# Postponed GpSimd and ScalarE work, and seven runs of unread bf16 products on TensorE

## The reference

```
x = x + gnn0(layernorm(x), adj)     # cosine scores of all pairs, tanh, exp, times adj, rows normalised, times x, times W
x = x + ffn0(layernorm(x))          # 16 experts, the two best per token, silu(x w1) * (x w2), times w3
x = x + gnn1(layernorm(x), adj)     # two steps of top-p attention, below
x = x + ffn1(layernorm(x))          # routed by the mean of all tokens, two of 8 experts, gelu, layer norm
```

```
R = (adj + I) / rowsum;  Xf = Xa = X
for n in range(2):
    q, k  = Xa @ W1.T @ W2.T, Xa @ W3.T
    probs = softmax(q @ k.T)                  # 2048 x 2048
    A     = the largest probs of each row up to a sum of 0.9, renormalised
    Xf, Xa = R @ Xf, A @ Xa
    Z    += Xf @ U1[n].T + Xa @ U2[n].T
out = layernorm(X + Z) * ln_g + ln_b
```

## Time and profile before

| what | value |
|---|---|
| median of 3 runs | 877.64 us (876.28 to 877.75) |
| the profiled execution's own time | 879.34 us |
| its span | 877.6 us |
| PE busy | 718.9 us, 82% |
| PEld busy | 530.0 us, 60% |
| DVE busy | 665.1 us, 76% |
| ACT busy | 484.5 us, 55% |
| POOL busy | 277.1 us, 32% |
| mean granted clock of PE | 0.911 of full speed |

### The profile page before, as it was taken

The page is one execution under the profiler, slowest core; times in us unless marked ns, Lnnn a source line. Parts: engine busy times, 40 slices in busy tenths (PEclk is TensorE's granted clock), DMA queues, the critical chain, the costliest instruction groups (busy, mean ns, idle before and its releaser), DMA issues.

```text
span 877.6 us, 15527 instructions
## 1 busy us (share of the span) xinstructions
PE 718.9 (82%) x5089; PEld 530.0 (60%) x5091; DVE 665.1 (76%) x2281; ACT 484.5 (55%) x723; POOL 277.1 (32%) x584
## 2 busy tenths in 40 slices
PE   4999999768999566799999989678778797886294
PEld 2455555427999543477777678465345675786263
DVE  6758677733444377889983499999899999999757
ACT  4877686304555326456555276467696775822153
POOL 3410421336666305400000034051432576770000
PEclk9999999787999869799999999797998997988788
DMA  8764000075887400000000000000000001101001
GB/s 152 118 98 77 26 17 10 26 172 154 230 229 236 160 1 1 0 2 1 1 1 2 1 1 2 1 2 1 0 1 1 1 2 47 51 1 33 0 1 48
DMA packets 47367, 41.94 MB, mean 48 GB/s; under 512 B 7376, under 2 KB 44112, under 8 KB 47280
## 3 DMA queue, kind: packets, MB, share of 16 engines
q1 hardware_dynamic: 29488, 19.95, 8.2%
q0 software_dynamic: 11456, 14.62, 8.0%
q10 hardware_dynamic: 6336, 6.32, 3.0%
HBM read 39.69 MB, written 9.57 MB: 56 GB/s over the span
## 4 chain that ended last, share of the span: by engine, by line
DVE 34%; PE 20%; issue 4%; ACT 4%; POOLq 1%; DVEq 1%; POOL 0%; ACTq 0%
DVE big L1595 6%; PE bank L2138 5%; PE bank L2042 5%; DVE cand L1513 4%; PE bank L2121 4%; DVE rm L1353 3%; DVE hacc L1508 3%; DVE big L1584 2%; DVE cand L1359 2%; DVE cand L1534 2%; PE bank L2315 2%; DVE big L1581 2%; DVE top L1529 2%; ACT big L1868 1%; PE bank L2327 1%
## 5 line engine op out<-in xcount | busy, mean ns | idle before, releaser
L2121 PE MATMUL bank<-ident,big 128*128 128x128 f32 x512 | 82.6, 311 | 31.3 <-DVEq L1618 21.9
L1868 ACT ACTIVATE big<-bank 128x512 f32<-128x512 f32 x128 | 71.0, 597 | 52.5 <-PE bank L2121 51.7
L2121 PEld LDWEIGHTS bank<-ident,big 128*128 128x128 f32 x512 | 63.3, 157 | 59.1 <-DVEq L1618 22.9
L2042 PE MATMUL bank<-kk,qq 64*128 64x512 f32 x256 | 78.8, 734 | 19.8 <-ACT big L1838 19.2
L1838 ACT ACTIVATE big<-bank,negm 128x2048 f32<-128x2048 f32 x32 | 62.7, 1958 | 47.1 <-DVE fsc L1645 36.8
L2049 PEld LDWEIGHTS bank<-parts,adjT 128*128 128x128 bf16 x1536 | 86.6, 98 | 3.0 <-issue 2.1
L2049 PE MATMUL bank<-parts,adjT 128*128 128x128 bf16 x1536 | 87.9, 219 | 0.6 <-DVE xn L1438 0.6
L1595 DVE SCALAR_TENSOR_TENSOR big<-big,st 128x2048 f32<-128x2048 f32 x32 | 75.2, 2388 | 5.2 <-PE bank L2121 5.2
L399 POOL DMA_INDIRECT ys_scratch<-big,parts x62 | 60.0, 967 | 33.2 <-ACT big L754 23.4
L844 PE MATMUL bank<-big,xn 128*128 128x512 f32 x128 | 62.2, 608 | 5.7 <-DVE big L546 5.7
L828 PE MATMUL bank<-xnT 128*128 128x512 f32 x128 | 62.0, 609 | 2.3 <-DVE xnT L535 2.3
(11 more groups left out here) (380 smaller groups left out, 1517.4 us busy)
## 6 DMA issues: line engine op xcount, KB each, us to landing
big<-in_L_ffn_w_dram SPq DMA_DIRECT2D x93, 128.0 KB
big<-in_adj_dram POOLq DMA_DIRECT2D x8, 512.0 KB, 7.3
big<-xs_scratch ACTq DMA_DIRECT2D x31, 132.0 KB
kk<-in_adj_dram POOLq DMA_DIRECT2D x4, 512.0 KB, 8.1
qq<-in_adj_dram POOLq DMA_DIRECT2D x4, 512.0 KB, 10.0
xs_scratch<-hacc SPq DMA_DIRECT2D x9, 132.0 KB
xs_scratch<-hacc ACTq DMA_DIRECT2D x8, 132.0 KB
res<-in_x_dram SPq DMA_DIRECT2D x4, 256.0 KB, 6.3
```

Of the source, the lines that this page charges most:

```text
L1868: nc.scalar.activation(MT[:, 4 * q:4 * q + 4, s * P:(s + 1) * P], bank[:, 5 + q % 2, :].rearrange("p (j i) -> p j i", j=4), ACT.Copy).then ...
L2042: nc.tensor.matmul(bank[:, c, :], qq[lo:lo + DA, (g * G + s) * P:(g * G + s + 1) * P], kk[lo:lo + DA, c * CH:(c + 1) * CH], start=True, st ...
L2121: mm = nc.tensor.transpose(bank[:, 5 + q % 2, j * P:(j + 1) * P], mk[:, s, jt * P:(jt + 1) * P], ident[:, :])
```

## The change

It has two parts.

**Postponed work.** `load_y(act, 1)` stands behind ACT's copies of the weights and ahead of that of the row sums. POOL's split of quarter `q` waits for both flags of group `q` as well, and its additions of `lnb` for those of group 4 (tiles 0 to 7) and group 5 (tiles 8 to 15). `take_pv(g)` waits for the quarter that it overwrites, no longer for all four.

**Unread products.** `keep_busy(b, times)` multiplies the bf16 identity with 512 columns of the bf16 adjacency into bank `b`, over and over; nobody reads the result. It is called seven times, 135 products in all.

```
+        def keep_busy(b, times):
+            for _ in range(times):
+                nc.tensor.matmul(bank[:, b, :], identb[:, :], adjT[:, 0, 0:CH], start=True, stop=True)
...
                 take_y(MB - 1)
-                load_y(act, 1)
                 ch.link(nc.scalar.activation(rs[:, 0:1], ones[:, 0:1], ACT.Exp))
...
+                load_y(act, 1)
                 act.wait_ge(rsum_done, NC + 1)
...
                 mm.then_inc(rsum_done, 1)
+                pe.wait_ge(y_out, 2 * MB)
+                pe.wait_ge(c_id, NT + 1)
+                keep_busy(7, 18)
...
                     pool.wait_ge(ab_part, 3 * q + 3)
+                    pool.wait_ge(flags_up, 2 * (q + 1))
...
                 for t in range(NT):
+                    if t % (NT // 2) == 0:
+                        pool.wait_ge(flags_up, 2 * (NC + 1 + t // (NT // 2)))
                     nc.gpsimd.tensor_tensor(res[:, t, :], res[:, t, :], lnb[:, :], ALU.add).then_inc(c_resb, 1)
...
                 def take_pv(g):
-                    if g == 0:
-                        act.wait_ge(ab_fin, NC)
+                    if g % 2 == 0:
+                        act.wait_ge(ab_fin, g // 2 + 1)
...
+                keep_busy(7, 14)
                 for c in range(NC):
                     turn_x(0, c)
...
                 make_ab(3)
+                pe.wait_ge(ab_part, 3 * 3)
+                keep_busy(4, 13)
                 logits(0, 1, 1)
                 flag_sum(0)
+                keep_busy(4, 12)
...
                         turn_h(1)
+                        keep_busy(2, 20)
                     if g < NG:
                         flag_sum(NG + g)
...
-                for i in range(2, len(XS)):
+                for i in range(2, len(XS) - 1):
                     turn_h(i)
+                keep_busy(6, 34)
+                turn_h(len(XS) - 1)
...
+                keep_busy(6, 24)
                 pe.wait_ge(d_w1, 4)
                 up(0)
```

## The result

| | before | the change |
|---|---|---|
| median, us (runs) | 876.96 (4; 875.99 to 877.75) | 869.40 (4; 866.73 to 871.06) |
| ratio, 95% interval | | 0.991, 0.989 to 0.993 |
| profiled execution, us; its span | 879.34; 877.6 | 871.06; 869.3 |
| mean granted clock of PE | 0.911 | 0.936 |
| PE busy, of the span | 718.9 (82%) | 743.8 (86%) |

The kernel became faster, by 7.6 us, where 8.9 were worked out and 868.7 was forecast. PE is busy for longer, since it now does unread work, in a shorter span. Lines of the code lie a little further down after the change (masking L1605 for L1595, logits L2052 for L2042, turns of masks L2131 for L2121, `turn_x` L2032, router L2324, up-products L2332); L295 is `keep_busy`.

The account below looks back on a forecast made before the run. PE's clock, low after idle holes, was taken to bound stretches of the chain. Terms 1.6 + 3.0 + 2.5 + 0.3 + 0.3 + 1.2 = 8.9 us gave 868.7 for the median, own case 866.5 to 871, with rivals 1 to 4 865.0 to 872.8.

Parts of the forecast that it names:

- Postponed work: First group of step 0: POOL's split waits for the flags, so DVE's masking is no longer slowed; 3.0 us gained.
- K7: 24 unread products ahead of the up-products, to run these warm: 2.0 us if on time, 1.2 taken.
- K2: 14 unread products at the start of block 2, ahead of `turn_x`: logits start earlier, 1.6 us taken.
- K1: 18 unread products at the end of block 1: hidden behind DVE's work; at most 7.7 us lost without that cover.
- K3 and K4: Unread products, 13 and 12, in the first group of step 0: PE stays warm for transposes and logits; 2.5 us gained.
- K5 and K6: Unread products in the last group's hole and ahead of `turn_h(4)`: both hidden, 0.3 us gained by each.
- Step 1: The clock falls at every group's flags, by chance a little earlier or later: 1.5 us either way.
- the second (lapses in both gaps): Rival: the clock lapses at the worst moment, K2 and K7 end late; 6.2 us gained, 871.4; chance 0.15.
- the first (clock holds): Rival: the clock holds everywhere, all upper ends; 10.5 us gained, 867.1; chance 0.12.
- The third: Rival: POOL's moved work collides with DVE in other groups and returns the 3.0 us; 871.7; chance 0.08.
- The fourth: Rival: transposes keep no clock, so K2 gives 0.9 us instead of 1.6; 869.4; chance 0.02.
- the fifth: Rival: unread products run cold and push the work behind them; 17 us slower, 894.6; chance 0.03.

Follow-up runs that it names:

- e3: The changed kernel without K3 and K4; 872.33 us, ratio 0.9946 to the kernel before.
- e4: The changed kernel with `load_y` back ahead of the table load, K1 kept; 872.76 us, ratio 0.9954 to the kernel before.
- e1: The changed kernel without its seven runs of unread products, postponed work kept; 873.29 us, ratio 0.9969 to the kernel before.
- e5: The changed kernel without K1 and K2; 887.59 us, ratio 0.9938 to the kernel before on the same chip.
- e2: The changed kernel with POOL's split and `take_pv`'s wait as before, all unread products kept; 871.62 us, ratio 0.9936 to the kernel before.
- e6: The changed kernel without K6 and K7; 888.49 us, ratio 0.9939 to the kernel before on the same chip.
- e9: The changed kernel again, unaltered, for a second profile; 886.59 us, ratio 0.9910 to the kernel before on the same chip.
- e10: The kernel before again, unaltered, for a second profile; 893.59 us, ratio 0.9993.
- e8: The changed kernel with 20 unread f32 transposes in place of K2's 14 products; 887.98 us, ratio 0.9936 to the kernel before on the same chip.

## Why the prediction was right, and where it was off

- **Price of a product**: 0.22 warm (K7's 24 in 5.34), and 0.44 cold (e3's K2, 14 in 6.10) for an estimate of 0.43.
- **The move of `load_y`** costs nothing and hides K1: right, and e4 shows what it would have been without, 4.9 us of waiting.
- **K2, 1.6**: 1.73 and 1.30 between the two pairs of profiles. The size was right and its cause only partly: against the profiles without K2, e1 and e5, the change gains 0.5, and the rest stands open. That the term was met is in part luck. That K2 begins cold and ends late was foreseen; e3 shows it eating its whole gain.
- **Postponed work, 3.0**: the total of e1 is 3.0, but 1.1 of it comes from the clock's rise behind it. It is 2.0 by the rows of e1 and by e3 against before, and 1.85 by e2. The 8.09 us did become 5.18 in the change, but the last 0.9 of that needs K3, as the prediction itself said ("Logits must not be late in its place").
- **K3 and K4, 2.5**: 3.3 by e3 and, beside POOL's work as before, 3.4 by e2; 2.25 by e1, whose clock rose early. So the split between the two terms was off by about 1 us and their sum was not. Both together with the postponed work 5.37 and 5.17, for 5.5.
- **K5 and K6, 0.6**: 0.49 and 0.43 in the two profiles of the change, 0.8 in the others. e6 puts it nearly all down to K5; the prediction gave half to each.
- **K7, 1.2**: 0.34 and 1.59 in the two profiles of the change, 1.95 in six others. The term was a compromise between a late and a punctual K7, and both happen; by the records of the clock K7 ran cold for 5.6 us in the first profile and for 3.4 in e9, the two ends that the prediction gave; the upper end, 2.0, is the common case, and the late end was named in the prediction (1.7 late; 1.49 measured in the first profile).
- **Step 1, nothing either way, 1.5 by chance**: it cost 1.99 in the first profile of the change and 0.3 to 3.2 over all versions without products there, never a gain. The forecast took before's step 1 as a typical one; eleven profiles of other versions, all between 217.15 and 220.14, say that its 216.90 is at the good end. The falls themselves are there: in before ten low stretches of 3.4 to 10.2 us begin between 551 and 801 us, from the first flag sum of step 1 to the last, for eight groups.

The sum is near for a reason that is partly luck. In the first profile the terms of the change came out at 7.9 (1.73 + 5.37 + 0.49 + 0.34), a punctual K7 would have made them 9.9 (0.85 and 1.95 for the last two, as in e2 to e4), and step 1 took 2.0 away: 5.9 are left. The profile shows 8.25, because 2.27 came from block 1, for which the prediction has no term; the profiled execution of before lay 2.4 over its median of 876.96. In the second pair (e10 and e9) the terms came out at 8.5, step 1 took 0.4, and the ratio of the medians is again 0.991. So 7.6 for 8.9 is the terms of the change, nearly as forecast, less a loss in step 1 that differs from one execution to the next. The forecast of 868.7 was also counted from 877.64, the median of three runs of before; with the fourth it is 876.96.

Of the rivals, the second (lapses in both gaps) is what the first profile shows at K7, the first (clock holds) what most others show there. The third is out: POOL's rows beside the row maxima stayed at 1.15, and the stretch from group 2 of step 0 to step 1 did not move by 0.1 us. The fourth is out by e8, the fifth by the rows of K3 and K4.

## What to carry to other kernels

Unread products that held the clock were worth their place only where the engine that waited behind them had nothing else to do: 41 us less of low clock in step 1 gave 2 to 5 us, because VectorE was busy for 95% of the time there (68.3 of 72 us in the windows above). Before pricing a slow instruction by the chain of waits, look at the idle time of the engine that waits for it. And a run of products should be sized so that it ends on time at the low clock, or have a predecessor close before it: 5.12 us of idle time lay ahead of e3's K2, which took 6.10 us and gave nothing, and 0.30 ahead of e4's, which took 3.18. One profile of a version was off by up to 3.4 us by where the falls lay, so take a second before believing a difference of that size.

## What was not expected of the hardware

The same kernel took 876.9, 890.5 and 894.4 us on different chips. Between the first chip and the one of e10, nearly all of it has come about by the end of block 1's expert products: the last of them ends at 290.75 and at 303.14. In the DMA row of the page (GB/s by slice, before and e10) the slices in which the expert weights are fetched are slower, 229 to 236 in slices 11 to 13 for 182 to 202. That the chip's memory is the cause is not shown by anything more.

```profile
GB/s 152 118 98 77 26 17 10 26 172 154 230 229 236 160 1 1 0 2 1 1 1 2 1 1 2 1 2 1 0 1 1 1 2 47 51 1 33 0 1 48
```

```profile
GB/s 164 106 96 74 25 19 7 26 195 173 186 202 182 125 98 1 0 1 2 1 1 1 1 1 3 1 1 0 1 1 1 1 2 12 85 1 32 0 1 47
```

Behind that point the chips agree to 0.2 us in every stretch in which the clock's falls lie alike (38.75 and 38.54, 216.90 and 216.71, 49.77 and 49.77).
